# Moving the weighted sums of a graph-network kernel into two bursts per batch

## The reference, cut to what matters

```python
hi = x @ W1[:H];  hj = x @ W1[H:]
h = relu(hi[:, :, None, :] + hj[:, None, :, :] + b1)   # every pair (i, j): 128 features
y = layernorm(h @ W2 + b2) * gamma + beta              # over the 128 features
o = einsum('bij,bijh->bih', adj, y)                    # the weighted sums
x1 = layernorm(x + o)
e = exp(si[:, :, None] + sj[:, None, :] + a_b) * adj   # si, sj: linear in x1
x2 = layernorm(x1 + (e / e.sum(2)) @ x1)
```

## Time and profile before

| | |
|---|---|
| median of 3 runs | 2622.48 us (2622.45 to 2622.6) |
| profiled execution, first to last instruction (its span) | 2621.4 us |
| PE matmul busy | 2577.0 us, 98% |
| PE weight loads busy | 2049.5 us, 78% |
| DVE busy | 2337.8 us, 89% |
| ACT busy | 2332.6 us, 89% |
| POOL busy | 1999.1 us, 76% |
| pair matmuls L529, 16384 | 1991.3 us |
| weighted-sum matmuls L573, 4096 | 545.9 us |
| mean granted TensorE clock | 0.998 of full |

### The profile page before, as it was taken

The page is one execution under the profiler, slowest core; times in us unless marked ns, Lnnn a source line. Parts: engine busy times, 40 slices in busy tenths (PEclk is TensorE's granted clock), DMA queues, the critical chain, the costliest instruction groups (busy, mean ns, idle before and its releaser), DMA issues.

```text
span 2621.4 us, 77145 instructions
## 1 busy us (share of the span) xinstructions
PE 2577.0 (98%) x21263; PEld 2049.5 (78%) x21263; DVE 2337.8 (89%) x18135; ACT 2332.6 (89%) x3650; POOL 1999.1 (76%) x1163
## 2 busy tenths in 40 slices
PE   8999999999999999999999999999999999999997
PEld 7777777777777777777777777777777777777774
DVE  7889988989899889998898989988988999989897
ACT  7899899899998998989989889999899898998996
POOL 7777777777777777777777777777777777777773
PEclk9999999999999999999999999999999999999999
DMA  0000000000000000000000000000000000000000
GB/s 17 8 12 7 11 7 10 11 6 11 11 6 11 6 11 11 6 11 11 6 11 6 11 11 6 11 10 7 11 6 11 11 6 11 8 8 11 6 7 7
DMA packets 48051, 23.49 MB, mean 9 GB/s; under 512 B 6208, under 2 KB 47808, under 8 KB 47808
## 3 DMA queue, kind: packets, MB, share of 16 engines
q1 hardware_dynamic: 46512, 21.12, 2.9%
q10 hardware_dynamic: 1296, 0.20, 0.0%
HBM read 17.11 MB, written 4.19 MB: 8 GB/s over the span
## 4 chain that ended last, share of the span: by engine, by line
PE 58%; DVE 24%; issue 11%; ACT 6%; POOL 0%; ACTq 0%; DVEq 0%; DMA 0%
PE y_ps L529 42%; DVE squares L517 16%; PE agg_ps L573 12%; DVE q L517 3%; ACT y L263 3%; DVE x1e L488 2%; ACT h L281 1%; ACT L334 1%; PE prep_ps L529 1%; PE tail_ps L529 1%; DVE o_sb L455 1%; PE tail_ps L584 1%; PE att_ps L529 1%; DVE eT L509 0%; DVE si_cols L499 0%
## 5 line engine op out<-in xcount | busy, mean ns | idle before, releaser
L252 POOL TENSOR_TENSOR h<-bT,aT 128x1024 f32<-128x1024 f32 x1024 | 1951.1, 1919 | 584.3 <-PE y_ps L529 572.9
L529 PEld LDWEIGHTS y_ps<-w_pair,h 128*128 128x128 f32 x16384 | 1885.7, 192 | 313.0 <-DVE q L517 260.3
L529 PE MATMUL y_ps<-w_pair,h 128*128 128x128 f32 x16384 | 1991.3, 278 | 21.9 <-DVE q L517 9.3
L517 DVE CUSTOM_DVE_ANT_0 squares<-y_ps,y 128x128 bf16<-128x128 f32 x8192 | 1842.3, 282 | 185.0 <-ACT y L263 171.2
L263 ACT ACTIVATE y<-y_ps 128x508 f32<-128x508 f32 x2048 | 1162.4, 595 | 190.8 <-PE y_ps L529 173.9
L281 ACT ACTIVATE h<-h 128x1024 f32<-128x1024 f32 x1024 | 1085.3, 1060 | 10.2 <-POOL h L252 10.2
L517 DVE DVE_READ_ACCUMULATOR2_ANT q<- 128x1 f32 x8192 | 659.1, 80 | 0.0
L573 PE MATMUL agg_ps<-y,wz 128*32 128x512 f32 x4096 | 545.9, 606 | 1.7 <-DVE o_sb L455 1.7
L573 PEld LDWEIGHTS agg_ps<-y,wz 128*32 128x32 f32 x4096 | 81.1, 108 | 66.7 <-issue 3.1
L492 DVE CUSTOM_DVE_ANT_0 s_terms<-x1e,v1row 128x128 f32<-128x128 f32 x64 | 99.5, 1554 | 0.1
L334 ACT ACT_TABLE_LOAD x64 | 82.1, 1283 | 4.3 <-DVE sj L504 3.2
(11 more groups left out here) (90 smaller groups left out, 740.4 us busy)
## 6 DMA issues: line engine op xcount, KB each, us to landing
x_in<-in_x_dram SPq DMA_DIRECT2D x64, 64.0 KB, 1.8
adj_in<-in_adj_dram SPq DMA_DIRECT2D x64, 64.0 KB, 1.9
x_res<-in_x_dram SPq DMA_DIRECT2D x64, 64.0 KB, 1.8
adj_res<-in_adj_dram SPq DMA_DIRECT2D x64, 64.0 KB, 1.9
out_dram<-x_out SPq DMA_DIRECT2D x64, 64.0 KB, 1.6
w<-in_L_gnn_W_dram ACTq DMA_DIRECT2D x1, 64.0 KB, 2.4
w1a<-in_L_gnn_W_dram SPq DMA_DIRECT2D x1, 64.0 KB, 2.2
w1b<-in_L_gnn_W_dram SPq DMA_DIRECT2D x1, 64.0 KB, 2.3
```

What stands on the lines that cost most here:

```text
L252: nc.gpsimd.tensor_tensor(h[:, u % HRING].rearrange("k (r g) s -> k r g s", g=GROUPS), bT[:, p, :].unsqueeze(1).unsqueeze(1).broadcast_to( ...
L517: last = nc.vector.tensor_tensor_reduce(out=squares[:, k % YRING, n, :], in0=y_ps[k % YRING][:, n, :], in1=y[:, p, i, :], scale=1.0, scala ...
L529: return nc.tensor.matmul(dst, lhsT, rhs, start=start, stop=stop)
```

## The change

- The eight chunks of a batch become two bursts of four, both in the slot after the batch: chunks 0 to 3 after unit 7, chunks 4 to 7 after unit 13. None is left for the slot after that.
- POOL makes `wz` at unit 6, not 8.
- ACT: the copy of the transposed `o_sb` at unit 6, not 7; the copies for the next batch at unit 7, not 8. The two waits of L344 and L346, for the sums that still read `y`, become one at quad 0 for all eight chunks.
- DVE: the row sum of the adjacency at (8, 0), not (6, 0), `x_beta` at (8, 1), not (7, 0), `project` at (8, 0), not (10, 0). The pair (u, e) is the half quad e of unit u ahead of which a step stands.
- PE: the transpose of `o_sb` at unit 5, not 6; the product with `w_back` at unit 7, not 8; the projections behind the quads of unit 7 (ahead of the burst), not ahead of those of unit 9.

```diff
--- before.py
+++ after.py
@@ -56,10 +56,8 @@
 
     CHUNK = 4
     CHUNKS = GROUP // CHUNK
-    WEIGHTS_UNIT = 4
-    POOL_WEIGHTS_UNIT = 8
-    CHUNK_STEP = UNITS // CHUNKS
-    EARLY_CHUNKS = (UNITS - WEIGHTS_UNIT) // CHUNK_STEP
+    POOL_WEIGHTS_UNIT = 6
+    BURST = {7: range(0, CHUNKS // 2), 13: range(CHUNKS // 2, CHUNKS)}
 
     ctx = ExitStack()
     with ctx:
@@ -309,13 +307,13 @@
                         if early >= 4:
                             act.wait_ge(rs2_ready, t - 3)
                         nc.scalar.activation(sd2[:], mv2[:, 1:2], ACT.Sqrt, bias=epsc[:, 0:1]).then_inc(sd2_ready, 1)
-                    if tail and u == 7:
+                    if tail and u == 6:
                         act.wait_ge(oT_ps_s, t - 1)
                         if early >= 3:
 
                             act.wait_ge(f_ps_s, t - 2)
                         copy(oT_sb[:], tail_ps[:, 0, :]).then_inc(oT_sb_s, 1)
-                    if prep and u == 8:
+                    if prep and u == 7:
                         prep_copies(t + 1, early + 1)
                         copy(adjT[:, 1 - p, :], prep_ps[:, 1, :]).then_inc(adjT_sb_s, 1)
                     if tail and u == 10:
@@ -341,8 +339,6 @@
                         for k in range(u * QPU, (u + 1) * QPU):
 
                             if k == 0 and early >= 2:
-                                act.wait_ge(agg_done, (t - 2) * CHUNKS + EARLY_CHUNKS)
-                            if k == EARLY_CHUNKS * CHUNK and early >= 2:
                                 act.wait_ge(agg_done, (t - 1) * CHUNKS)
                             if k == 0 and early == 0:
 
@@ -456,10 +452,10 @@
                                                        in1=o_sb[:], op0=ALU.mult, op1=ALU.add).then_inc(
                                                            o_stored if e == CHUNK - 1 else o_part, 1)
 
-                    if tail and (u, e) == (6, 0):
+                    if tail and (u, e) == (8, 0):
                         dve.wait_ge(xres_loaded[p], nth16(half, p, -2) * 2)
                         nc.vector.reduce_sum(adj_sum[:], adj_res[:, p, :], axis=mybir.AxisListType.X).then_inc(adj_sum_ready, 1)
-                    if tail and (u, e) == (7, 0):
+                    if tail and (u, e) == (8, 1):
                         dve.wait_ge(adj_sum_ready, t - 1)
                         nc.vector.scalar_tensor_tensor(out=x_beta[:], in0=beta_rows[:], scalar=adj_sum[:, 0:1], in1=x_res[:, p, :],
                                                        op0=ALU.mult, op1=ALU.add).then_inc(x_beta_ready, 1)
@@ -475,7 +471,7 @@
 
                         dve.sem_inc(s_passed, 1)
                         nc.vector.bn_aggr(mv1[:], st1[:]).then_inc(mv1_ready, 1)
-                    if prep and (u, e) == (10, 0):
+                    if prep and (u, e) == (8, 0):
                         if early >= 1:
 
                             dve.wait_ge(u_ready, t * UNITS)
@@ -579,16 +575,14 @@
                     if finish and u == 0:
                         pe.wait_ge(eT_ready, t - 2)
                         mm(att_ps[:, 0:K + 1], eT[:], x1e[:]).then_inc(att_done, 1)
-                    if tail and u == 6:
+                    if tail and u == 5:
                         pe.wait_ge(o_stored, t - 1)
                         nc.tensor.transpose(tail_ps[:, 0, :], o_sb[:], ident[:]).then_inc(oT_ps_s, 1)
                     if prep and u == 6:
                         prep_transposes(t + 1, 1 - p, nth16(half, p, 1), True)
-                    if tail and u == 8:
+                    if tail and u == 7:
                         pe.wait_ge(oT_sb_s, t - 1)
                         mm(tail_ps[:, 1, :], oT_sb[:], w_back[:]).then_inc(f_ps_s, 1)
-                    if prep and u == 9:
-                        prep_products(t + 1)
                     if tail and u == 13:
 
                         pe.wait_ge(si_ready, t - 1)
@@ -603,18 +597,16 @@
                             for n in range(QUART):
                                 last = mm(y_ps[k % YRING][:, n, :], h[:, u % HRING, (k % QPU) * QUART + n, :], w_pair[:])
                             last.then_inc(y_in_psum, 1)
-                    chunk = (u + 1 - WEIGHTS_UNIT) // CHUNK_STEP - 1
-                    chunk_due = (u + 1 - WEIGHTS_UNIT) % CHUNK_STEP == 0
-                    if gather and chunk_due and chunk >= 0:
-                        if chunk == 0:
-
-                            pe.wait_ge(w_ready, t)
-                            if early >= 2:
-                                pe.wait_ge(o_stored, t - 1)
-                        weighted_sums(1 - p, chunk)
-                    if tail and chunk_due and chunk < 0:
-
-                        weighted_sums(p, chunk + CHUNKS)
+                    if prep and u == 7:
+                        prep_products(t + 1)
+                    if gather and u in BURST:
+                        for chunk in BURST[u]:
+                            if chunk == 0:
+
+                                pe.wait_ge(w_ready, t)
+                                if early >= 2:
+                                    pe.wait_ge(o_stored, t - 1)
+                            weighted_sums(1 - p, chunk)
 
             run_slots(pe, slot)
 
```

## The result

The changed kernel takes 3128.21 us (median of 4 runs, 3124.21 to 3128.38) against 2622.51: a ratio of 1.192, 95% interval 1.191 to 1.194. I had forecast 2816, at most 2890. The direction was right; of the 505.7 us, called 505 from here on, the forecast has 193.

The account below looks back on a forecast made before the run. PE leads, but DVE and ACT have under 4 us idle a slot. Stretches sum to 43.23 against 40.23: +3.00 a slot, +3.26 after the loop's jump, 193 over slots 2 to 63, giving 2816 us; range 2690 to 2890.

Parts of the forecast that it names:

- The chunks themselves: PE's chunk work: a burst of four takes 3.58 us, two bursts 7.16 against 8.00, so 0.84 less a batch.
- The price of a switch: PE changing between quads and chunks: a chunk costs 1.00 us alone, 0.86 further in a row, so 0.14 per switch.
- Quads 16 to 26: PE's stretch after the first burst, paced by DVE: 11.60 us against 12.38, two chunks gone, PE waiting 2.2.
- Quads 28 to 0: Slot's end to the next quad 0: 4.99 us less its chunk, 3.99, the exponential done in the burst.
- 0 to 12: Slot's head, paced by ACT and DVE: 14.16 us against 14.89; behind the loop's jump 0.62 more.
- Quads 26 to 28: Two quads and the second burst: 1.88 + 3.58 = 5.46 us against 2.98.
- a rival at 0.12: PE's waits lower the clock: 2946 us, or 2881 if only every second slot falls; chance 0.12.
- The waits on `o_sb`: PE holds quads 10 and 11 for the transpose of `o_sb` at unit 5: 1.4 us more.
- for quad 4 to 8: Slot's head: DVE starts quad 4 late after ACT's copy, so PE waits 1.1 us for quad 8.
- the early transpose: Moving the transpose of `o_sb` to unit 5 costs about 0.8 of the 1.4 us wait.
- the nothing for `wz`: POOL's `wz` at unit 6 makes unit 6's relu input about 1 us late, DVE being behind anyway: no cost.
- The faster rival: Switches decide on PE: six fewer at 0.14 over 62 slots give 52 us, 2570 us; chance 0.07.

Follow-up runs that it names:

- singles: Changed kernel, seven DVE steps reading an operand from PSUM, its bursts dealt as eight single chunks after units 7 to 14: 2774.89 us.
- pairs: With seven DVE steps reading PSUM: changed kernel, two chunks each after units 7, 9, 11, 13, 2697.56 us; kernel before, after 1, 6, 10, 14, 2529.52 us.
- the run with four steps freed: Changed kernel with v, x_beta, si_cols and eT each reading one operand from PSUM in place of SBUF: 2779.57 us, ratio 1.060.
- the versions with freed steps: Changed kernel with DVE steps reading an operand from PSUM: four steps 2779.57 us; seven, adding x1e and both score sums, 2700.72 us.
- all freed in both orders: Seven DVE steps reading an operand from PSUM: changed kernel 2700.72 us; kernel before, x_beta also one unit later, 2585.08 us.
- the run with spare matmuls: Changed kernel with four spare 128x128 matmuls on PE ahead of quads 4, 10, 20 and 26, result unused: 3048.67 us, ratio 1.162.

## Why the prediction was wrong

*The chunks themselves* were right: 3.58 forecast for a burst, 3.57 measured. The price of a switch was not: 0.14 in my sum, 0.33 in the rows of the singles and pairs. As DVE sets the pace of the long stretches, little of this reaches the sum.

*Quads 16 to 26* is the step that failed most plainly. I wrote "`x_beta` comes in, 0.41" and took DVE's 9.82 us from the earlier trace rows as work that moves unchanged. A good part of it was holding: 5.1 us of the slot before go to seven steps that need 2.4 when nothing holds them. After the change they take 8.9. The stretch is 13.59 in place of 11.60; in the run with four steps freed it is 11.01, with the first score sum still held.

*Quads 28 to 0 and 0 to 12* were off for the same reason: eT (1.47) delays the attention product, v (1.83) what follows. The 14.16 for a slot without the loop's jump measured 14.55; the 14.78 for a slot behind it measured 16.84, DVE's late start and the held v coming together there, and the clock with them.

*Quads 26 to 28*: 5.46 forecast, 7.17 measured, the lowered clock. I had this as a rival at 0.12, with the right sign; it is true in part, 80 us, but as a consequence of the holds and not by itself: the versions with freed steps wait 1.6 and 1.3 us in a row, where I forecast 1.1 and 1.4, and stay at 0.997.

*The sum without the new holds and the clock* came near: 193 forecast, 157 in the run with four steps freed, 116 with all freed in both orders. Some of that is luck: in the first of these x1e and the second score sum are 1.3 us a slot shorter than in my sum, which I did not foresee. The waits on `o_sb` (1.4 forecast, 1.28 to 1.29 measured) and for quad 4 to 8 (1.1 forecast, 1.57 in the rows of the pairs and 0.54 more) stood where I put them. Of the 0.8 for the early transpose 0.54 was found, but not as a gain in time; the nothing for `wz` was right.

*The faster rival* failed as argued, since PE's waits grew. But it had a core: four switches fewer gave 56 us where the chunks stay spread, as the pairs show.

My check "DVE busy time unchanged at 36.5" points straight at it: DVE's 229 us more are 3.6 a slot. And the trace of before had the sign, unread. Two groups of DVE with the same operation and shape:

```profile
L488 DVE TENSOR_SCALAR x1e<-x1p,mv,rs 128x128 f32<-128x128 f32 x64 | 60.6, 947 | 0.1
...
L444 DVE TENSOR_SCALAR x_out<-x2p,mv,rs 128x128 f32<-128x128 f32 x64 | 23.0, 359 | 0.1
```

Here one form of instruction with two durations was one that waited for something.

## What to carry to other kernels

When small steps on DVE run beside long GpSimd instructions, compare the durations of equal forms before you move anything: where they differ, the longer one may be waiting inside the instruction, and then it won't keep its length in another place. Give such a step an operand in PSUM, or cut the GpSimd instruction. Grouping PE's odd work saves its switches, but it is also what covers the stretches in which other engines set the pace: leave a share of it in each of them.

## What the runs showed that I had not expected

- A DVE step of 0.28 to 0.41 us takes up to 1.95 us when a GpSimd add is under way; DVE's squares, with one operand in PSUM, are never held (0.28 us in every kernel here).
- Behind waits in a row of 2.40 us and 0.28, or one of 3.25, TensorE's granted clock fell from 2.4 towards 1.2 GHz in most slots of this kernel, not in all (0.56 in the 3 us from 1537.00); in the run with four steps freed, with waits of up to 1.9, 0.5 and 1.3 us, the mean stays at 0.997. The Trainium skill, TensorE: Matmul & The Clock Gate, on the HAM clock gate, has idleness as the cause of a lowered clock, and the run with spare matmuls agrees: 0.957 to 0.987.
- Spare matmuls made a kernel faster by 80 us.
- In the rows above a switch from the quads' matmuls to a chunk and back costs 0.33 us, of which only 0.14 shows on the chunk's side; the other 0.19 comes once for each run of quads, of two or of four.
